# State-space layer: the kept part of x scaled by GpSimd instead of ScalarE

## The reference

```
x = x + layer(_layernorm(x))

layer(h):                                # h is the normalised x
    u  = h * rsqrt(mean(h*h) + 1e-6) * norm_weight
    Bu = u @ real(B_bar).T + 1j * (u @ imag(B_bar).T)
    xs = scan(x_t = Lam_bar * x_{t-1} + Bu_t)      # along the positions
    y  = 2 * (real(xs) @ C_re.T - imag(xs) @ C_im.T) + D * u
    return h + y
```

## Time and profile before

| | us |
|---|---|
| median of 3 runs | 2141.83 |
| lowest, highest | 2141.06, 2143.85 |
| profiled execution | 2146.78 |
| its span in the trace | 2145.0 |

### The profile page before, as it was taken

The page is one execution under the profiler, slowest core; times in us unless marked ns, Lnnn a source line. Parts: engine busy times, 40 slices in busy tenths (PEclk is TensorE's granted clock), DMA queues, the critical chain, the costliest instruction groups (busy, mean ns, idle before and its releaser), DMA issues. The chain is left out here.

```text
span 2145.0 us, 67400 instructions
## 1 busy us (share of the span) xinstructions
PE 1917.1 (89%) x27305; PEld 1301.6 (61%) x27305; DVE 1589.6 (74%) x3679; ACT 1503.0 (70%) x4403; POOL 506.6 (24%) x605
## 2 busy tenths in 40 slices
PE   3888888887899999999979976879999999997998
PEld 1444444443576766667757864547667776776786
DVE  6899999996477787877865654637777777786553
ACT  3899899994677777776644549757777777664453
POOL 2000000000243343334331100024344343433110
PEclk9999999999999999999999997989999999999998
DMA  6655555540000000000001000000000000000211
GB/s 184 158 118 128 126 122 125 124 92 1 11 22 12 22 12 22 13 22 12 22 15 39 2 1 1 1 11 22 12 22 13 22 13 22 12 22 13 55 31 35
DMA packets 71782, 91.88 MB, mean 43 GB/s; under 512 B 8889, under 2 KB 64574, under 8 KB 67678
## 3 DMA queue, kind: packets, MB, share of 16 engines
q1 hardware_dynamic: 70322, 87.14, 17.4%
q10 hardware_dynamic: 1152, 0.43, 0.1%
HBM read 39.67 MB, written 31.10 MB: 33 GB/s over the span
## 5 line engine op out<-in xcount | busy, mean ns | idle before, releaser
L448 ACT ACTIVATE r_pr<-r_dist,k_negc 128x512 f32<-128x512 f32 (+1 forms) x512 | 369.2, 847 | 18.3 <-PE r_dist L337 12.4
L1245 POOL TENSOR_TENSOR f1l_pn<-f1l_p,f1l_rs 128x512 f32<-128x512 f32 (+1 forms) x256 | 206.7, 829 | 350.3 <-DVE f1l_rs L1044 350.3
L1245 POOL TENSOR_TENSOR f2l_pn<-f2l_p,f2l_rs 128x512 f32<-128x512 f32 (+1 forms) x256 | 206.8, 829 | 345.3 <-DVE f2l_rs L1044 345.3
L351 PE MATMUL r_acc<-r_pr,r_vp 128*32 128x128 f32 (+2 forms) x3584 | 204.7, 342 | 30.5 <-DVE r_pr L537 19.2
L974 ACT ACTIVATE f1l_p<-f1l_sm,f1l_nb 128x192 f32<-128x192 f32 x512 | 208.8, 417 | 1.6 <-DVE f1l_nb L1037 1.5
L974 ACT ACTIVATE f2l_p<-f2l_sm,f2l_nb 128x192 f32<-128x192 f32 x512 | 208.6, 417 | 1.5 <-DVE f2l_nb L1037 1.5
L529 DVE SCALAR_TENSOR_TENSOR r_pr<-r_pr,k_lo,r_cap 128x512 f32<-128x512 f32 x256 | 179.9, 744 | 11.1 <-ACT r_pr L448 10.8
L537 DVE TENSOR_SCALAR r_pr<-r_pr,k_hi,k_lo 128x768 f32<-128x768 f32 x256 | 163.7, 674 | 4.9 <-ACT r_pr L448 2.5
L1037 DVE TENSOR_REDUCE f2l_nb<-f2l_sm 128x4 f32<-128x768 f32 x128 | 121.8, 952 | 50.5 <-PE f2l_sm L857 47.6
L1037 DVE TENSOR_REDUCE f1l_nb<-f1l_sm 128x4 f32<-128x768 f32 x128 | 121.6, 951 | 43.6 <-PE f1l_sm L857 41.6
L825 PE MATMUL f1l_pj<-f1l_xt,k_wqkv 128*128 128x512 f32 x244 | 136.9, 643 | 2.8 <-ACT f1l_kt L956 0.4
(11 more groups left out here) (414 smaller groups left out, 4720.0 us busy)
## 6 DMA issues: line engine op xcount, KB each, us to landing
rbf_rows<-r_part SPq DMA_DIRECT2D x112, 128.0 KB, 2.0
r_qs<-rbf_rows SPq DMA_DIRECT2D x30, 384.0 KB
r_ks<-rbf_rows SPq DMA_DIRECT2D x30, 384.0 KB
f1l_vs<-f1l_vv SPq DMA_DIRECT2D x32, 256.0 KB, 3.9
f2l_vs<-f2l_vv SPq DMA_DIRECT2D x32, 256.0 KB, 3.9
rbf_rows<-r_part SPq DMA_DIRECT2D x16, 384.0 KB, 2.6
rbf_rows<-r_part SPq DMA_DIRECT2D x16, 256.0 KB, 2.9
out<-k_x SPq DMA_DIRECT2D x16, 256.0 KB, 2.3
```

Source lines behind the costliest of these rows:

```text
L351: mm = nc.tensor.matmul(acc[32 * g:32 * g + 32, q0:q0 + n], vp[:, par, t, g, 32 * q:32 * q + 32], pr[:, (PAIRS * b + 2 * q + g // 2) % RIN ...
L448: nc.scalar.activation(pr[:, n % RING, e, cols], dist[:, e, cols], ACT.Exp, scale=K["negc"][:, h:h + 1]).then_inc(done, 1)
L1245: ins = nc.gpsimd.tensor_tensor(pn[:, u % 2, at:at + HU * w].rearrange("p (k c) -> p k c", k=HU), p[:, u % 2, :, cols], r.broadcast_to([P, ...
```

## The change

The function `kept` moves from ScalarE's queue to GpSimd's. Each ACTIVATE becomes a `tensor_scalar` with a multiplication and an addition, with the same two scalars per partition, in place on the same tile. GpSimd does the tiles of pair 0 at the start of the stage, and those of pair q + 1 behind addition q. It has to wait for s_un, because `rows` on ScalarE reads the same tiles that `kept` overwrites; on ScalarE the order of the queue saw to that. VectorE's `residual` waits for s_h as before.

```
--- before.py
+++ after.py
@@ scalar
-            def kept(q):
-                for j in range(2 * NT):
-                    t = 2 * NT * q + j
-                    ins = a(K["x"][:, t, :], K["x"][:, t, :], ACT.Identity, scale=h1[:, t:t + 1], bias=h0[:, t:t + 1])
-                ins.then_inc(s_h, 1)
...
-                if 0 <= p + 3 < N:
-                    kept(p + 3)
@@ gpsimd
+            def kept(q):
+                pool.wait_ge(s_un, q + 1)
+                for j in range(2 * NT):
+                    t = 2 * NT * q + j
+                    ins = nc.gpsimd.tensor_scalar(K["x"][:, t, :], K["x"][:, t, :], h1[:, t:t + 1], h0[:, t:t + 1],
+                                                  ALU.mult, ALU.add)
+                ins.then_inc(s_h, 1)
+
+            kept(0)
             for q in range(N):
                 pool.wait_ge(s_r, q + 1)
                 wait(pool, s_s, q)
                 nc.gpsimd.tensor_tensor(wi[:], t1[:], t2[:], ALU.add).then_inc(s_w, 1)
+                if q + 1 < N:
+                    kept(q + 1)
```

## The result

| | before | after |
|---|---|---|
| median, us | 2142.11 | 2132.31 |
| lowest to highest | 2140.86 to 2144.59 | 2130.9 to 2137.91 |
| ratio, 95% interval | | 0.9959 (0.9945 to 0.9972) |

The change is faster by 0.41%, or 8.8 us; 2135 had been forecast, and the time lies in the stated range. The profiled execution after spans 2129.7 us, 15.3 less than the one before. That is more than the change is worth, and the trace says how much more.

What follows compares the result with a forecast made beforehand. ScalarE's order was taken to bound the state-space layer's start and ScalarE its full pairs, TensorE's loop the early ones; -6.2 - 1.7 + 1.2 = -6.7 us, from the median 2141.83 to 2135 us, range 2131 to 2153.

Steps and rivals of the forecast that it cites:

- The start: First rotation of the state-space layer: two kept blocks no longer stand ahead of leave 0 on ScalarE, -6.2 us.
- The early pairs: Early spacings between rotations: ScalarE's work falls from 7.15 to 4.1 us a pair, but no gain is taken.
- +1.2 for contention: Early pairs 1 to 2 and 2 to 3: GpSimd and VectorE hold each other at SBUF, +1.2 us in all.
- TensorE's loop of 6.65 stays: Early pairs: inputs 3.68, turn 1.97 and ScalarE's leave 1.0 nearly give the 6.84 us spacing, also after the change.
- The form of the contention: Scan and two multiplications: VectorE waits one tile before each, 1.2 us; GpSimd's queue grows about 2.5, to 7.1 a pair.
- The full pairs: Late spacings: 5 to 6 falls from 11.40 to about 9.7 us, -1.7; 4 to 5 and 6 to 7 stay.
- TensorE's clock: Window 1330 to 1336, clock granted 0.72: costs some 1.7 us, left in; if gone, another -1.7.
- The tile, t = 0.41: One 128x128 TENSOR_SCALAR on GpSimd: 0.41 us, from a line through 512- and 256-column multiplications; 3.3 us a block.
- A: GpSimd's kept block: a dearer tile, 0.6 to 0.78 us, gives 2138 to 2142 us; chance 0.13.
- B: Addition q + 1 behind block q + 1: GpSimd becomes the bound with tiles above 0.78 us, 2142 to 2165; chance 0.17.
- C: Scan q behind block q + 1: VectorE waits for all eight tiles, some 8 us lost, 2137 to 2147; chance 0.17.
- The signs: Profile after: leave 0 at 1293.4, rotation 0 at 1298.4, tile row 0.41 us, full spacings 9.6 to 9.8, stage about 113.

Runs made afterwards that it cites:

- kept_first_two: Against the kernel before, only kept 0 and 1 go to GpSimd, kept 2 to 7 stay on ScalarE; ratio 0.9980 of before.
- kept_out: Against the changed kernel, the scaling of x is left out and a tiny memset signals in its place; stage 108.3 us.
- before_again: The unchanged kernel before, profiled once more; stage 118.8 us.
- rows_later: Against the changed kernel, ScalarE copies the first transposed result ahead of rows, not behind it; rotation 7 is 3.5 us earlier.
- kept_early: Against the changed kernel, GpSimd does kept 1 before addition 0; early spacings 1.7 us less, rotation 7 only 0.2 us earlier.
- kept_twice: Against the changed kernel, GpSimd computes each kept tile twice, once into scratch; +6.0 us on after, 0.9984 of before.
- kept_memset: Against the changed kernel, scaling left out, GpSimd writes 8 scratch tiles of 432 columns per pair instead; block 3.25 us, scan mean 1.60 us.

## Why the prediction was right, and where its steps were off

- *The start, -6.2:* measured -6.15, confirmed alone by kept_first_two.
- *The early pairs, "I take nothing here", and +1.2 for contention:* both sizes are off and offset each other in part. Without any block the three spacings fall by 2.4 us (kept_out), and the failed step is "TensorE's loop of 6.65 stays". No such loop set these pairs: before, ScalarE did, with its 7.15 us a pair, and TensorE waited 2.26 us for leave 1. The sum of 6.65 came near 6.84 by luck; it took turn 0's 1.97 us for turn 1, which took 1.19, and left the wait out. With ScalarE relieved, VectorE's queue is the bound, 5.14, 6.26 and 7.40 us in kept_out. The block takes 1.8 of the 2.4 back. The net is -0.5, where I had +1.2.
- *The form of the contention:* I had VectorE waiting for up to a tile before each of three instructions. Its scan rose by 0.08 us in the mean, the multiplication L1709 from 0.687 to 0.697. GpSimd was held, by 2.0 us a block; I had entered that too, as 2.5. My queue of 7.1 us a pair measures 6.7 (1.27 + 5.45), and what it did was to make an addition 1.5 us late where the spacing is short (idle 2.89 instead of 1.38), and nothing where it is 9.6.
- *The full pairs, -1.7:* measured -2.3 over the spacings 3 to 6. The failed part is "4 to 5 was at TensorE's round and stays". In the earlier trace rows 9.81 was short only because outputs 2 before it had been slow; before_again shows ScalarE's beat, 11.39 twice. After the change the second is 10.93, not 9.7: rows in front of the copy of the result still hold TensorE (rows_later). That -1.7 and -2.3 lie near each other is partly luck: 1.8 of the 2.3 came at the spacing 4 to 5 (11.39 to 9.60), where nothing was taken.
- *TensorE's clock, "if it is gone, it is another -1.7":* it was gone in both profiles of after (12.95 and 12.96), and in before_again too. But before the change it had cost nothing, since ScalarE was the bound behind it; only with ScalarE relieved does it cost 1.6 us (kept_out, kept_early).
- *The tile, t = 0.41:* 0.43. The line through two sizes of another operation was good enough. *A* and *B* were ruled out by this. kept_twice tests B's formula at 0.86 us: it has the pair nearly right (10.7 us, where the additions come every 10.1) and the edge wrong. It gives a kernel 4 us slower than before (11.6 lost against 7.9), and kept_twice is still 3 us faster by rotation 7, since the gain without a block was more than 7.9 and the full pairs lost nothing in all (+0.5 and -0.5), where the formula has 1.0 each. At t = 0.41 this formula loses 0.4 us, where the forecast's own term is +1.2: the two do not join. The edge lies above 0.86, not at 0.78.
- *C* did not happen between the tiles and the scan, but did in kept_memset.
- *The signs:* leave 0 and rotation 0 came where they were said to (10.39 and 15.42 us behind the start of the stage). Two others would have misled: the mean of the TENSOR_SCALAR row is above 0.6, through the stretched tiles, and in the early pairs the addition does not wait for s_t but follows the block at once, the sign of B, though the block costs the two spacings only 1.7 and 0.15 us.
- The sum of the three terms is -6.7 forecast, -9.0 measured; what the first two profiles differ by beyond that, 6.3 us, is the tail (2.6) and pieces outside the stage (4.1), less 0.3 behind the last score.

## What to carry to other kernels

Moving work off a full engine pays first where it stands ahead of the first link of a pipeline: two blocks at the start gave 6.2 of 9.0 us, though the six others took three times as much work off the engine. A spacing that looks as if it were at the next engine's bound may be the echo of a long one before it; take the beat over several. When the load has moved, look again at what the lightened queue still has in front of the work others wait for: swapping two steps gave another 3.5 us in this stage.

## What had not been expected of the hardware

- A GpSimd TENSOR_SCALAR that reads SBUF is stretched from 0.44 to 1.41-1.50 us beside VectorE's scan and multiplications (kept_twice). In the rows above these keep their 1.23 and 0.69 us even when the tile started first; in after the scan was held too, by 0.2 us at most. In the earlier trace rows VectorE was the one held (1.31 instead of 0.40). "SBUF — State Buffer" in the Trainium skill, section Who interferes with whom, gives the ports to whoever starts first; the second of these traces agrees, the first does not, at least by the recorded starts.
- In kept_memset, GpSimd memsets, which read nothing, held an 8-column TENSOR_SCALAR of VectorE's for 2.31 us, until the last of the queued memsets was through. Beside the tiles that read x the same instruction lasted 0.40 us at most.
